# Fewer parts of q and k before the first head; the rest, a split of gate weights and a set of zeros among the heads

## The chip, the cores and the metric

One core of one Trainium2 chip. The metric is the device time of one execution in microseconds. A core's engines are TensorE (PE in the rows, with its weight loads as PEld), VectorE (DVE), ScalarE (ACT), GpSimd (POOL) and SyncE (SP), which here only issues DMA.

## The reference

Two layers, each attention-like mixing and then a feed-forward part, on x and a context of 8 batches of 256 rows by 256 columns. The change lies in the first mixing. Its q is the normalised x, its k and v are the context, with 8 heads of 32 columns:

```python
gate_in = jnp.concatenate([q, k, v], axis=-1)
ig = jnp.transpose(gate_in @ igate_w.T + igate_b, (0, 2, 1))
fg = jnp.transpose(gate_in @ fgate_w.T + fgate_b, (0, 2, 1))
log_f_cum = jnp.cumsum(jax.nn.log_sigmoid(fg), axis=-1)
log_fg_mat = log_f_cum[:, :, :, None] - log_f_cum[:, :, None, :]
log_D = jnp.where(ltr, log_fg_mat + ig[:, :, None, :], -jnp.inf)
max_log_D = jnp.max(log_D, axis=-1, keepdims=True)
D = jnp.exp(log_D - max_log_D)
qk = jnp.einsum('bhsd,bhtd->bhst', qh, kh) / jnp.sqrt(jnp.float32(dh))
C = qk * D
normalizer = jnp.maximum(jnp.abs(jnp.sum(C, axis=-1, keepdims=True)), jnp.exp(-max_log_D))
h = jnp.einsum('bhst,bhtd->bhsd', C / (normalizer + EPS_BACKEND), vh)
```

h is then normalised by head and added to x. Behind it come a mixture of 32 experts (4 a row) with a shared one, a long convolution of the context with two small feed-forward blocks, and 8 dense experts of four times that width.

## The kernel before

The first mixing is 64 heads, batch by batch (head i is head i % 8 of batch i // 8). For exactness q and k are taken as a high part (rounded to fp32r) and a low part (the rest). The tile `parts` holds both, of k first and then of q in the same place, in four groups of 512 rows, which are two batches or 16 heads each; a group has two halves c of 128 columns. ScalarE makes the high parts of k, VectorE those of q (line 566), GpSimd all low parts by a subtraction (line 1618). SyncE stores each finished group to HBM (`k_parts`, `q_parts`), and loads it back as stacks: one stack holds, for four heads, high, low, high of k beside high, high, low of q on 96 partitions, in six DMAs (`load_stack`, line 439), so that one matrix product (lines 1795 and 1796) gives the scores. A group makes four stacks, so 16 stacks in all; `stackA` and `stackB` hold two each. `stackB` lies where q transposed (`qT`) is kept, and the second half of `stackA` where the gates' weights are.

Ahead of the heads the opening normalises x (line 556), transposes context and x (TensorE, lines 1750), multiplies by the gates' weights (line 1756), and forms from the gates the rows of cumulated log gates on VectorE and ScalarE (lines 569 to 584, `rows_done` at the last). TensorE fills its wait with 42 products of no use (`spare`, line 1743), then transposes these rows (line 1783) and starts head 0.

In a head TensorE makes scores (lines 1795 and 1796) and the exponents' argument (line 1801), ScalarE the exponentials `Dm` (lines 1308 and 1309), VectorE the product of both `Cm` (line 645), and TensorE two heads later the values (lines 1810 to 1812). The scores of head i wait for `Cm` of head i - 2. VectorE has small work between products: `head_work` closes the batch before, GpSimd finishes it.

All DMAs of SyncE stand in one queue in program order. Through the heads they are the stacks and, between them, 16 stores of zeros (`slots_in`, line 461), which clear 12.6 MB of HBM for the experts' slots from two rows of `eS` that GpSimd set to zero at the start (line 1600). VectorE waits for the last of them behind its last product. `split_gates` (lines 588 to 596) splits weights that are first read behind the heads.

## Time and profile before

| | |
|---|---|
| median of 3 runs | 1803.57 us (1801.59 to 1806.38) |
| the profiled execution: time, span | 1809.64 us, 1807.6 us |
| busy: PE, DVE, ACT, POOL | 92%, 67%, 26%, 25% |
| mean granted TensorE clock | 0.959 |
| first scores of head 0, last of head 63 | 57.44 us, about 151 us |
| DMA, whole span | 127.49 MB, 71 GB/s |

The chain that ended last lies for 78% on TensorE and 39% on one line of the dense experts (1943), which the change does not touch. The opening and the heads are the first 155 us of the span. A clock of 1.00 in the rows is 2.4 GHz, 0.50 is 1.2 GHz. A row with xN merges N operations; its time goes from the first's start to the last's end.

### The profile page before, as it was taken

The page shows a single profiled execution, that of the slowest core. Times are in us where ns is not written, and L with a number is a line of the kernel's source. Part 1 is how long each engine was busy: PE and PEld are TensorE (multiplying, and loading weights), DVE is VectorE, ACT ScalarE, POOL GpSimd, SP SyncE. Part 2 cuts the span into 40 slices and gives each one's busy share as a digit, 9 for nine tenths or more (in the row PEclk, how much of TensorE's full clock was granted, in tenths as well). Part 3 has the DMA queues.
Part 4 walks back from the last instruction along what each step waited for, and adds up shares of the span by engine and source line. Part 5 has one row for each costly group of instructions (what it writes and reads, how often), then busy time and mean ns, then how long its engine had stood idle before and what let it go on. Part 6 is the DMA issues. An engine that isn't in the chain of part 4 may idle for free.

```text
span 1807.6 us, 28969 instructions
## 1 busy us (share of the span) xinstructions
PE 1665.6 (92%) x9720; PEld 1429.5 (79%) x9721; DVE 1209.2 (67%) x2472; ACT 478.8 (26%) x844; POOL 452.3 (25%) x299
## 2 busy tenths in 40 slices
PE   5998987698956698999999999999999999999998
PEld 5796663398844588888888888888888888888887
DVE  7556778566655695666676676676676676666765
ACT  3455331143422365321111121121211111211211
POOL 5152256688436511010010010010010110100100
PEclk9998998899977898999999999999999999999999
DMA  7992021378643200001000000010000010010001
GB/s 239 294 328 88 24 83 75 105 243 264 204 136 101 64 1 18 18 18 36 18 27 25 17 35 17 17 35 17 17 35 17 17 35 17 17 35 17 17 0 47
DMA packets 72002, 127.49 MB, mean 71 GB/s; under 512 B 8320, under 2 KB 51776, under 8 KB 71808
## 3 DMA queue, kind: packets, MB, share of 16 engines
q1 hardware_dynamic: 38096, 84.31, 14.3%
q10 hardware_dynamic: 27696, 25.51, 4.4%
q0 software_dynamic: 6144, 16.79, 2.9%
q8 instruction: 42, 0.69, 0.2%
q14 instruction: 24, 0.20, 0.0%
HBM read 82.54 MB, written 44.04 MB: 70 GB/s over the span
## 4 chain that ended last, share of the span: by engine, by line
PE 78%; DVE 7%; issue 4%; POOL 4%; DMA 4%; ACT 2%; another core or an unknown queue 1%; SPq 0%; POOLq 0%; DVEq 0%; ACTq 0%
PE ps L1943 39%; PE ps L1959 20%; PE ps L2050 4%; DMA slots_in<-xn,idS 2%; POOL slots_in L1672 2%; PE ps L2069 2%; PE ps L2125 1%; PE ps L1743 1%; PE ps L2147 1%; PE ps L2030 1%; DMA x<-in_x 1%; PE ps L1812 1%; PE ps L1811 1%; PE ps L2059 1%
## 5 line engine op out<-in xcount | busy, mean ns | idle before, releaser
L1943 PE MATMUL ps<-xTH,wH 128*128 128x512 f32 x1024 | 402.8, 393 | 1.6 <-DVE hF L1197 1.6
L1943 PE MATMUL ps<-xTH,wL 128*128 128x512 f32 x1024 | 402.2, 393 | 0.0
L1943 PE MATMUL ps<-xTL,wH 128*128 128x512 f32 x1024 | 399.1, 390 | 0.0
L1345 ACT ACTIVATE sg<-ps 128x512 f32<-128x512 f32 x264 | 157.9, 599 | 885.8 <-PE ps L1943 878.0
L1197 DVE TENSOR_TENSOR hF<-sg,ps 128x512 f32<-128x512 f32 x256 | 175.7, 686 | 304.0 <-ACT sg L1345 304.0
L1644 POOL TENSOR_TENSOR wL<-wS,wH 128x1536 fp32r<-128x1536 f32 x32 | 111.9, 3496 | 961.0 <-ACT wH L1340 961.0
L1959 PE MATMUL ps<-wL,hH 128*128 128x256 f32 x1024 | 289.8, 283 | 0.0
L1959 PE MATMUL ps<-wH,hL 128*128 128x256 f32 x1024 | 289.7, 283 | 0.0
L1959 PE MATMUL ps<-wH,hH 128*128 128x256 f32 x1024 | 288.6, 282 | 0.5 <-DVE hL L1206 0.5
L1206 DVE TENSOR_TENSOR hL<-hF,hH 128x512 fp32r<-128x512 f32 x256 | 258.0, 1008 | 0.1
L1943 PEld LDWEIGHTS ps<-xTL,wH 128*128 128x128 f32 x1024 | 192.8, 188 | 42.2
L1216 DVE SCALAR_TENSOR_TENSOR x<-ps,cw,x 128x256 f32<-128x256 f32 x512 | 222.6, 476 | 1.0 <-PE ps L1959 1.0
L1943 PEld LDWEIGHTS ps<-xTH,wH 128*128 128x128 f32 x1024 | 193.8, 189 | 35.6 <-ACT sg L1345 1.5
L1943 PEld LDWEIGHTS ps<-xTH,wL 128*128 128x128 f32 x1024 | 193.9, 189 | 30.5
L1959 PEld LDWEIGHTS ps<-wH,hH 128*128 128x128 f32 x1024 | 195.5, 191 | 10.6 <-DVE hL L1206 0.7
L1959 PEld LDWEIGHTS ps<-wH,hL 128*128 128x128 f32 x1024 | 195.5, 191 | 9.9
L1959 PEld LDWEIGHTS ps<-wL,hH 128*128 128x128 f32 x1024 | 195.5, 191 | 0.0
L1200 DVE CAST hH<-hF 128x512 fp32r<-128x512 f32 x256 | 109.3, 427 | 36.9 <-PE ps L1959 28.2
L1672 POOL DMA_INDIRECT slots_in<-xn,idS x64 | 74.9, 1170 | 61.0 <-DMA slots_in<-xn,idS 31.2
L2050 PE MATMUL ps<-eHL,hH 128*128 x384 | 82.2, 297 | 2.3 <-POOL eHL L1659 2.3
L1743 PE MATMUL ps<-maskT,idb 128*128 128x384 bf16 x308 | 67.2, 345 | 15.4 <-DVE x L939 15.4
L1711 POOL DMA_INDIRECT yg<-slots_out,idG x48 | 49.3, 1027 | 73.8 <-DMA slots_out<-yo 49.1
(387 smaller groups left out, 2469.0 us busy)
## 6 DMA issues: line engine op xcount, KB each, us to landing
wS<-in_w SPq DMA_DIRECT2D x32, 768.0 KB
slots_in<-eS SPq DMA_DIRECT2D x16, 768.0 KB, 8.5
eS<-in_wr SPq DMA_DIRECT2D x32, 384.0 KB, 3.8
xl<-slots_in ACTq DMA_DIRECT2D x48, 256.0 KB, 3.6
slots_out<-yo ACTq DMA_DIRECT2D x48, 256.0 KB, 2.7
k_parts<-parts SPq DMA_DIRECT2D x8, 512.0 KB, 4.4
q_parts<-parts SPq DMA_DIRECT2D x8, 512.0 KB, 5.0
stackA<-k_parts SPq DMA_DIRECT2D x24, 128.0 KB, 6.4
```

The costliest lines, as they stand in the source:

```text
L1197: dve.tensor_tensor(hF[:, b, :], sg[:, b, :], ps[:, 2 + b, :], ALU.mult).then_inc(mul_done, 1)
L1200: dve.tensor_copy(hH[:, b, :], hF[:, b, :]).then_inc(h_high, 1)
L1206: dve.tensor_tensor(hL[:, b, :], hF[:, b, :], f32(hH[:, b, :]), ALU.subtract).then_inc(h_low, 1)
L1216: dve.scalar_tensor_tensor(x[:, tile, :], acc, cw2[:, tile, bass.ds(it, 1)], x[:, tile, :], ALU.mult, ALU.add).then_inc(evac_done, 1)
L1345: act.activation(sg[:, b, :], ps[:, b, :], ACT.Silu).then_inc(silu_done, 1)
L1644: pool.tensor_tensor(blocks(wL, slot, plain), blocks(wS, slot, plain), f32(blocks(wH, slot, plain)), ALU.subtract).then_inc(w_low, 1)
L1672: pool.indirect_dma_start(xs_d, bass.IndirectOffsetOnAxis(ap=idS[:, n, k:k + 1], axis=0), xn[:, n, :], None, bounds_check=TILES * P - 1, o ...
L1711: pool.indirect_dma_start(slot_rows(n)[:, k, :], None, ys_d, bass.IndirectOffsetOnAxis(ap=idG[:, n, k:k + 1], axis=0), bounds_check=TILES ...
L1743: pe.matmul(ps[:, bank, 0:384], idb[:, :], maskT[:, :], start=True, stop=True)
L1943: last = pe.matmul(ps[:, 2 * half + b, :], piece(w, s, slot, col, P), v[:, k, g * 512:(g + 1) * 512], start=q == 0, stop=q == 5)
L1959: last = pe.matmul(o, h[:, b, t * P:(t + 1) * P], piece(w, s, slot, col, D), start=(opens and t % 2 == 0 and q == 0), stop=(closes and q = ...
L2050: last = pe.matmul(ps[:, 2 + b, t * D:(t + 1) * D], h[:, b, (2 * t + k) * P:(2 * t + k + 1) * P], eFlat[:, bass.ds(off + (w + k * D), D)], ...
```

## The change

Before the first head, only group 0 of q and k gets its low parts: those of k on GpSimd, those of q on VectorE itself right after the casts. GpSimd makes the low parts of k of groups 1 to 3 when the gate rows are done, and then those of q. VectorE makes the high parts of q of groups 1 to 3 behind the products of heads 5, 6 and 7, each pair behind a wait for that group's k stores. Stacks 2 and 3 get places of their own, `stackC` in `xn` and `stackD` in `eS`, so all four stacks of group 0 can be loaded before q transposed is free. `eS` is therefore set to zero only when the scores of head 15 are done. `split_gates` moves behind the product of head 14 and two small operations behind that of head 15. The column of means in `vext` is made group by group. SyncE's order follows.

```diff
@@ -143,6 +143,8 @@
         parts = at("parts", [P, 2, 2, NT * P], F32R, start["dcw"])
         stackA = at("stackA", [P, 2, 2, 4, SEQ], F32R, start["wS"])
         stackB = at("stackB", [P, 2, 2, 4, SEQ], F32R, start["xTH"])
+        stackC = at("stackC", [P, 2, 4, SEQ], F32R, start["xn"] + 4 * 8 * D)
+        stackD = at("stackD", [P, 2, 4, SEQ], F32R, start["eS"])
         qT = at("qT", [P, 2, NT * P], F32, start["xTH"])
         kT = at("kT", [P, 2, NT * P], F32, start["xTL"])
         xTM = at("xTM", [P, 2, NT * P], F32R, start["ya"])
...
@@ -390,6 +392,8 @@
 
         def stack(j):
 
+            if j in (2, 3):
+                return (stackC, stackD)[j - 2][:, :, :, :]
             return (stackA, stackB)[j % STACKS // 2][:, j % 2, :, :, :]
 
         def f32(ap):
@@ -438,26 +442,35 @@
                         src = of[i, :, c, b * SEQ:(b + 1) * SEQ].rearrange("(h d) t -> d h t", d=DH)
                         sp.dma_start(f32(stack(j)[r * DH:(r + 1) * DH, a, :, :]), src).then_inc(stack_loaded[j % STACKS], 16)
 
-            for g in range(4):
+            sp.wait_ge(k_low, 2)
+            store_parts(kp_d, 0, k_stored[0])
+            sp.wait_ge(q_low, 2)
+            store_parts(qp_d, 0, q_stored[0])
+            load_stack(0)
+            sp.wait_ge(gates_done, 1)
+            load_stack(1)
+            load_stack(2)
+            load_stack(3)
+            for g in range(1, 4):
                 sp.wait_ge(k_low, 2 * g + 2)
                 store_parts(kp_d, g, k_stored[g])
-            for g in range(4):
+            for g in range(1, 4):
                 sp.wait_ge(q_low, 2 * g + 2)
                 store_parts(qp_d, g, q_stored[g])
-                if g == 0:
-                    load_stack(0)
-            sp.wait_ge(gates_done, 1)
-            for j in range(1, STACKS):
-                load_stack(j)
-
-            sp.wait_ge(vext_done, 1)
+                if g == 1:
+                    load_stack(4)
+                    load_stack(5)
+            load_stack(6)
+            load_stack(7)
+
+            sp.wait_ge(vext_done, 4)
             for t, n in ((FZ, "fz"), (FW, "fw"), (Win, "win"), (peT, "pet"), (Wp1, "wp1"), (Wp2, "wp2")):
                 sp.dma_start(t[tuple(slice(None) for _ in t.shape)], dram[n]).then_inc(conv_loaded, 16)
             sp.wait_ge(zero_done, 1)
             zv = xs_d.rearrange("(a p c) d -> a p (c d)", p=P, c=UW // D)
             for a in range(TILES * D // UW):
-                if STACKS + a < 2 * B:
-                    load_stack(STACKS + a)
+                if 2 * STACKS + a < 2 * B:
+                    load_stack(2 * STACKS + a)
                 sp.dma_start(zv[a], eS[:, 0:2, :].rearrange("p i c -> p (i c)")).then_inc(zeros_stored, 16)
 
             sp.wait_ge(pv_done, B * NH)
@@ -554,16 +567,28 @@
             link(row_scales(range(4)))
             for n in range(NT):
                 dve.tensor_scalar(xn[:, n, :], x[:, n, :], mv[:, n, 0:1], rs[:, n:n + 1], ALU.subtract, ALU.mult).then_inc(norm_done, 1)
-            for g in range(4):
-                last = dve.tensor_reduce(vext[:, 4 * g:4 * g + 4, :, DH + 1], vext[:, 4 * g:4 * g + 4, :, 0:DH], AXX, ALU.add)
-                if g == 3:
-                    link(last)
-                    dve.tensor_scalar(vext[:, :, :, DH + 1], vext[:, :, :, DH + 1], 1.0 / DH, None, ALU.mult).then_inc(vext_done, 1)
+
+            def query_high(g):
+
                 dve.wait_ge(k_stored[g], 32)
                 for c in range(2):
                     cols_ = slice(g * 512, (g + 1) * 512)
                     dve.wait_ge(mixT_copied, 8 + 2 * g + c + 1)
                     dve.tensor_copy(parts[:, 0, c, cols_], qT[:, c, cols_]).then_inc(q_high, 1)
+
+            def head_means(g):
+
+                means = vext[:, 4 * g:4 * g + 4, :, DH + 1]
+                link(dve.tensor_reduce(means, vext[:, 4 * g:4 * g + 4, :, 0:DH], AXX, ALU.add))
+                dve.tensor_scalar(means, means, 1.0 / DH, None, ALU.mult).then_inc(vext_done, 1)
+
+            head_means(0)
+            query_high(0)
+            for c in range(2):
+                dve.wait_ge(q_high, c + 1)
+                dve.tensor_tensor(parts[:, 1, c, 0:512], qT[:, c, 0:512], f32(parts[:, 0, c, 0:512]), ALU.subtract).then_inc(q_low, 1)
+            for g in range(1, 4):
+                head_means(g)
             dve.wait_ge(gates_copied, 1)
 
             dve.scalar_tensor_tensor(r1[64:, :], rg[64:, :], -1.0, rg[64:, :], ALU.mult, ALU.min).then_inc(negabs_done, 1)
@@ -596,9 +621,6 @@
                 dve.scalar_tensor_tensor(zHL[:, :], f32(zHL[:, :]), ident[0:2, 0:1], low, ALU.mult, ALU.add).then_inc(bias_split, 1)
                 dve.wait_ge(bias_split, 1)
 
-            split_gates()
-            dve.tensor_scalar(tc[:, 0:1], nl[:, 0:1], -0.5, None, ALU.mult)
-            link(dve.tensor_scalar(tc[:, 4:9], tilen[:, 0:5], float(RING), float(RING), ALU.mult, ALU.add))
 
             def constant(k, shape):
 
@@ -645,6 +667,13 @@
                 dve.scalar_tensor_tensor(Cm[:, i % 3, :], ps[:, i % 2, 0:384], float(DH) ** -0.5, Dm[:, i % 2, :],
                                          ALU.mult, ALU.mult).then_inc(mixed_done, 1)
                 b = i // NH
+                if 5 <= i < 8:
+                    query_high(i - 4)
+                if i == 14:
+                    split_gates()
+                if i == 15:
+                    dve.tensor_scalar(tc[:, 0:1], nl[:, 0:1], -0.5, None, ALU.mult)
+                    link(dve.tensor_scalar(tc[:, 4:9], tilen[:, 0:5], float(RING), float(RING), ALU.mult, ALU.add))
                 if i >= 8 and i % 8 in (2, 3):
                     head_work(b - 1, i % 8 - 2)
                 if i >= 16 and i % 8 == 1:
@@ -1597,7 +1626,6 @@
                 pool.wait_ge(pool_step, steps[0])
 
 
-            pool.memset(eS[:, 0:2, :], 0.0).then_inc(zero_done, 1)
             link(pool.memset(zcol[:, :], 0.0))
             pool.wait_ge(ident_loaded, 16)
             pool.tensor_copy(idb[:, :], ident[:, :])
@@ -1609,17 +1637,21 @@
                 for a in range(2):
                     last = pool.tensor_copy(gateW[:, :, b, 64 * a + 8 * b:64 * a + 8 * b + 8], gwt[:, 0:4, 8 * a:8 * a + 8])
             last.then_inc(gatew_done, 1)
-            def low_parts(src, first, signal):
-
-                for j in range(8):
+            def low_parts(src, copied, first, last, signal):
+
+                for j in range(2 * first, 2 * last):
                     g, c = j // 2, j % 2
                     cols_ = slice(g * 512, (g + 1) * 512)
-                    pool.wait_ge(q_high if first else k_high, j + 1)
+                    pool.wait_ge(copied, j + 1)
                     pool.tensor_tensor(parts[:, 1, c, cols_], src[:, c, cols_], f32(parts[:, 0, c, cols_]), ALU.subtract).then_inc(signal, 1)
 
-            low_parts(kT, 0, k_low)
-            low_parts(qT, 8, q_low)
+            low_parts(kT, k_high, 0, 1, k_low)
             pool.wait_ge(const_loaded, 11 * 16)
+            pool.wait_ge(rows_done, 1)
+            low_parts(kT, k_high, 1, 4, k_low)
+            low_parts(qT, q_high, 1, 4, q_low)
+            pool.wait_ge(qk_done, 16)
+            pool.memset(eS[:, 0:2, :], 0.0).then_inc(zero_done, 1)
 
             def rows_of(ap):
                 return ap.rearrange("p s h -> p (s h)").unsqueeze(2).to_broadcast([P, 2 * NH, DH])
@@ -1806,6 +1838,7 @@
                 o0, o1 = (ps[:, 4 + 2 * (b % 2) + s, h * (DH + 2):(h + 1) * (DH + 2)] for s in range(2))
                 pe.wait_ge(mixed_done, i + 1)
                 if h == 0:
+                    pe.wait_ge(vext_done, b // 2 + 1)
                     wait(pe, head_read, b - 1)
                 pe.matmul(o0, Cm[:, i % 3, P:2 * P], vext[:, 2 * b, h, :], start=True, stop=True)
                 pe.matmul(o1, Cm[:, i % 3, 2 * P:3 * P], vext[:, 2 * b, h, :], start=True, stop=False)
```

On VectorE, at the end of the opening, before (`parts<-qT` are casts to the high parts, `vext` the head sums, `r_129<-rg` the first gate operation):

```order
L558 TENSOR_REDUCE vext<-vext 128x32
L566 CAST parts<-qT 128x512 x2
L558 TENSOR_REDUCE vext<-vext 128x32
L566 CAST parts<-qT 128x512 x2
L558 TENSOR_REDUCE vext<-vext 128x32
L566 CAST parts<-qT 128x512 x2
L558 TENSOR_REDUCE vext<-vext 128x32
L561 TENSOR_SCALAR vext<-vext 128x128
L566 CAST parts<-qT 128x512 x2
L569 SCALAR_TENSOR_TENSOR r_129<-rg 64x256
```

On VectorE at the same place, now:

```order
L582 TENSOR_REDUCE vext<-vext 128x32
L583 TENSOR_SCALAR vext<-vext 128x32
L577 CAST parts<-qT 128x512 x2
L589 TENSOR_TENSOR parts<-qT,parts 128x512 x2
L582 TENSOR_REDUCE vext<-vext 128x32
L583 TENSOR_SCALAR vext<-vext 128x32
L582 TENSOR_REDUCE vext<-vext 128x32
L583 TENSOR_SCALAR vext<-vext 128x32
L582 TENSOR_REDUCE vext<-vext 128x32
L583 TENSOR_SCALAR vext<-vext 128x32
L594 SCALAR_TENSOR_TENSOR r_131<-rg 64x256
```

Three of the four pairs of casts are gone from there, and two subtractions have come. On VectorE in heads 0 to 10, now (before, `Cm` stood there eleven times with nothing between):

```order
L609 CAST MHL<-r_132 64x256
L667 SCALAR_TENSOR_TENSOR Cm<-ps,Dm 128x384 x6
L577 CAST parts<-qT 128x512 x2
L667 SCALAR_TENSOR_TENSOR Cm<-ps,Dm 128x384
L577 CAST parts<-qT 128x512 x2
L667 SCALAR_TENSOR_TENSOR Cm<-ps,Dm 128x384
L577 CAST parts<-qT 128x512 x2
L667 SCALAR_TENSOR_TENSOR Cm<-ps,Dm 128x384 x3
```

The casts stand behind the products of heads 5, 6 and 7. On SyncE, from the first store of parts on, now (before, all stores of k and q stood ahead of stack 1):

```order
L431 DMA k_parts<-parts 256x1x512 x2
L431 DMA q_parts<-parts 256x1x512 x2
L443 DMA stackA<-k_parts 32x4x256 x3
L443 DMA stackA<-q_parts 32x4x256 x3
L443 DMA stackA<-k_parts 32x4x256 x3
L443 DMA stackA<-q_parts 32x4x256 x3
L443 DMA stackC<-k_parts 32x4x256 x3
L443 DMA stackC<-q_parts 32x4x256 x3
L443 DMA stackD<-k_parts 32x4x256 x3
L443 DMA stackD<-q_parts 32x4x256 x3
L431 DMA k_parts<-parts 256x1x512 x6
L431 DMA q_parts<-parts 256x1x512 x2
```

Six stores of k and six of q have moved behind the loads of stacks 0 to 3.

## Rows read from the trace of the kernel before

**Rows 1.** Stretches of 5 us: busy PE, PEld, DVE, ACT, POOL; clock, DMA share, GB/s.
```profile
60.00:65.00 5.00, 4.94 (x37) 3.99 (x35) 2.23 (x4) 2.45 (x7) 0.00 (x0) 0.90 1.07 245
...
105.00:110.00 5.00, 5.00 (x43) 4.61 (x43) 2.44 (x5) 2.76 (x8) 0.06 (x1) 1.00 1.07 362
...
135.00:140.00 5.00, 5.00 (x43) 4.48 (x42) 3.31 (x11) 2.74 (x8) 4.77 (x4) 1.00 1.02 424
```

**Rows 2.** Timeline of the opening: start, us busy, engine, line, tiles, idle before and releaser.
```profile
36.18 1.21 DVE L558 TENSOR_REDUCE vext<-vext 128x32 f32<-128x1024 f32 x1
...
44.07 2.90 DVE L566 CAST parts<-qT 128x512 fp32r<-128x512 f32 x2
...
45.35 0.47 ACT L1264 ACTIVATE rg<-ps,gbias 128x256 f32<-128x256 f32 x1 [2.72 <-PE ps L1756]
...
47.00 1.38 DVE L569 SCALAR_TENSOR_TENSOR r<-rg 64x256 f32<-64x256 f32 x1
...
50.58 0.42 DVE L571 SCALAR_TENSOR_TENSOR r<-rg,r 64x256 f32<-64x256 f32 x1 [2.20 <-ACT r L1268]
...
55.59 0.28 DVE L584 CAST MHL<-r 64x256 fp32r<-64x256 f32 x1
...
57.44 0.67 PE L1795 MATMUL ps<-stackA 96*128 96x256 f32 x1
...
60.99 0.39 PE L1795 MATMUL ps<-stackA 96*128 96x256 f32 x1
```

**Rows 3.** Busy time by stretches of 1 us, before the first head.
```profile
51.00:52.00 1.00, 1.00 (x7) 0.49 (x5) 0.69 (x1) 0.24 (x1) 0.00 (x0) 1.00 1.05 404
52.00:53.00 1.00, 0.14 (x1) 0.00 (x0) 0.76 (x2) 0.98 (x2) 0.00 (x0) 1.00 1.05 401
...
54.00:55.00 1.00, 0.00 (x0) 0.00 (x0) 0.92 (x4) 0.00 (x0) 0.00 (x0) 0.57 1.03 393
```

**Rows 4.** Timeline: low parts on GpSimd, and a pair of casts.
```profile
19.84 9.84 POOL L1618 TENSOR_TENSOR parts<-kT,parts 128x512 fp32r<-128x512 f32 x8 [10.00 <-ACT parts L1258]
...
37.30 0.75 DVE L566 CAST parts<-qT 128x512 fp32r<-128x512 f32 x2
37.80 11.71 POOL L1618 TENSOR_TENSOR parts<-qT,parts 128x512 fp32r<-128x512 f32 x8 [8.12 <-DVE parts L566]
```

**Rows 5.** Timeline of the kernel's start.
```profile
0.73 1.38 POOL L1600 MEMSET eS<- 128x1536 f32 x1 [0.29 <-POOLq L2301]
...
1.31 0.87 DVE L541 CAST one<-ones 2x128 fp32r<-2x128 f32 x1
```

**Rows 6.** Timeline of heads 53 to 55.
```profile
136.15 0.36 PE L1795 MATMUL ps<-stackA 96*128 96x256 f32 x1
...
137.78 1.28 POOL L1635 TENSOR_TENSOR hC<-hC,bcv 128x512 f32<-128x512 f32 x1
...
138.06 0.56 DVE L645 SCALAR_TENSOR_TENSOR Cm<-ps,Dm 128x384 f32<-128x384 f32 x1 [0.81 <-PE ps L1796]
...
139.10 0.36 PE L1795 MATMUL ps<-stackA 96*128 96x256 f32 x1
```

**Rows 7.** Timeline: first and last operation of the gate weights' split, eight in all.
```profile
55.90 0.20 DVE L588 CAST wg0H<-wg 128x64 fp32r<-128x64 f32 x1
...
57.85 0.47 DVE L596 SCALAR_TENSOR_TENSOR zHL<-zHL,ident,cmp 2x256 fp32r<-2x256 f32 x1
```

**Rows 8.** Timeline of SyncE's queue.
```profile
41.01 1.18 SPq L427 DMA_DIRECT2D q_parts<-parts  x2
45.51 1.30 SPq L439 DMA_DIRECT2D stackA<-k_parts  x3
```

**Rows 9.** Page, DMA issues: KB each, median us from issue to landing.
```profile
slots_in<-eS SPq DMA_DIRECT2D x16, 768.0 KB, 8.5
```

**Rows 10.** Timeline behind the heads.
```profile
158.18 0.17 DVE L535 SCALAR_TENSOR_TENSOR sd<-mv,rs 128x8 f32<-128x8 f32 x1
...
162.63 0.62 ACT L1281 ACTIVATE hQ<-hC 128x512 f32<-128x512 f32 x1
```

More of the change, by code:

```diff
@@ L229, in build @@
         assert end["Cm"] <= start["tF"] and end["kc"] <= end["tF"] and end["h1T"] <= start["Dm"] and end["id2"] <= end["cw2"]
-        assert end["parts"] <= end["ya"] and end["stackA"] <= start["FW"] and end["stackB"] <= end["xTH"]
+        assert end["parts"] <= end["ya"] and end["stackA"] <= start["FW"] and end["stackB"] <= end["xTH"] and end["stackC"] <= end["xn"] and end["stackD"] <= end["eS"]
         assert end["hC"] <= end["xn"] and end["hQ"] <= start["Dm"] and end["GI"] <= end["vext"] and end["WF"] <= end["eS"]
```

## The prediction

> **What bounds the kernel.** I read the stretches first, then the timeline of the opening, then its releasers. Through the heads TensorE is full (4.94 of 5 us at first, then 5.00), while the DMA engines are busy too, at 245 GB/s for loads of the stacks alone, 362 for stack loads and stores of zeros in turn and 424 for zeros alone [rows 1]. So what can be won is an earlier first head, and nothing in the heads, where each microsecond that TensorE waits is lost. What sets the first head is seen in [rows 2]. The gates' sums are copied out by ScalarE at 45.35 to 45.82, but VectorE still casts the last parts of q until 46.97 and takes up the gates (L569) only at 47.00. That operation lasts 1.38 us, and the next of the same shape 0.42 (L571). The last row of the gate chain ends at 55.87, and the first scores start at 57.44.
>
> Why 1.38: GpSimd makes low parts until 37.80 + 11.71 = 49.51 [rows 4]. Its eight of k, with no VectorE cast beside them, took 9.84, 1.23 each. A pair of VectorE casts that started at 37.30, ahead of GpSimd's first operation at 37.80, took 0.75; the pair at 44.07, with GpSimd in full run, took 2.90, so 1.45 for one cast [rows 2, 4].
>
> **The opening after the change.** VectorE's order is: sum of the first head group (1.21, [rows 2]) with its scaling, two casts (0.75), two low parts of q (I take 0.6 each: 512 columns against 0.42 for 256 of L571), then three more sums with scalings. The norms end with the row at 36.18, which starts there. 36.2 + 1.2 + 0.2 + 0.75 + 1.2 = 39.6, then three times 1.4 is 43.9, ahead of 45.82. So L569 starts when the gates are copied: 47.00 - 45.85 = 1.15 us won. GpSimd has nothing to do then, so it lasts 0.42 instead of 1.38: 0.96 won. The rest of the chain, 48.38 to 55.87, starts after that or lies beside an idle GpSimd from 49.51, and stays as it is. The rows are ready at about 53.8.
>
> The granted clock of TensorE was 1.00 (2.4 GHz) at 51 to 52 us and 0.57 in 54 to 55 [rows 3], so it fell to 1.2 GHz there, and the 0.90 of 60 to 65 [rows 1] says that it rose again soon after 60; before it fell, TensorE had run out of filling work near 52.1 (0.14 us busy in 52 to 53 [rows 3]) and waited for the rows until 55.9, 3.7 us. The wait shrinks to 1.6 us. What that does to the clock no row tells; I take it as staying up (55 in 100). At 1.2 GHz the scores of heads 0 and 2 started at 57.44 and 60.99 [rows 2]; two heads at full speed take 2 x 1.474 = 2.95 instead of 3.55, so 0.6 won, and nothing if the clock falls all the same. First head: 2.1 earlier, 2.7 with the clock.
>
> The first stack is no bar: before, the q store issued at 41.01 let the load start at 45.51, 4.5 us [rows 8]; now 39.65 + 4.5 = 44.2, first scores at 55.
>
> **The heads' slack on VectorE.** From 136.15 to 139.10 TensorE does two heads, 1.474 each; the product of the head that starts at 136.15 ends at 138.62, and the head two later needs it at 139.10 [rows 6]. So VectorE has 1.474 - 0.56 = 0.91 us free in a head and may then be 0.48 late. The product itself kept 0.56 with a GpSimd operation of 512 columns running (137.78 to 139.06) [rows 6], so the low parts of k under the first heads cost the products nothing.
>
> **Casts in heads 5, 6, 7.** GpSimd makes k's six remaining low parts from 53.8 to 53.8 + 6 x 1.23 = 61.2. With the first scores at 55.0 (57.44 - 2.1, and 0.35 that I allow for the transposes at full clock), head 5's product ends at T = 55.0 + 5 x 1.474 + 2.47 = 64.8. Its pair of casts finds GpSimd idle: 0.75, inside 0.91. But each pair releases two low parts of q (2.5 us), which are running when head 6's product ends at T + 1.47. There casts and low parts take turns as in the pair of 2.90: the running one ends at T + 2.0, a cast to 2.3, a low part to 3.5, a cast to 3.9. Head 7's product ends at T + 4.5, not T + 2.95: 1.55 late, less 0.48, holds TensorE 1.07. The third pair goes likewise from T + 4.5 to T + 7.0; head 8's product ends at T + 7.6, not T + 4.4: 3.2 late, less 0.48 is **2.7 us** in all. Bounds: 0 if no cast is held; 3.5 if both pairs take the full 2.90. I take 2.7, worked from the row with both.
>
> A rule bears on this: the Trainium skill, SBUF — State Buffer, section Who interferes with whom, says that VectorE's casts in their two-port mode and GpSimd hold one shared port pair as a lock for a whole instruction, and that whoever issues first decides who is blocked. By that, casts that come first cost 0.75 a pair and GpSimd pays; the pair at 37.30 shows such a case, and it would bring the sum to that of the second rival below.
>
> **Split of the gate weights in head 14.** Eight linked operations, 55.90 to 57.85 + 0.47 = 58.32: 2.42 us [rows 7], before the change beside waiting and free. Now it stands between two products. And the zeros (one set of 1.38 us) are made by GpSimd when head 15's scores are done, some 0.6 after they start, so at S + 2.1 if head 14 starts at S, until S + 3.45; head 14's product ends at S + 2.47. At the start of the kernel a VectorE cast of 2 rows took 0.87 and ended at 2.18, just behind that same set (0.73 to 2.11) [rows 5]. So the split's first cast waits 1.0. 1.0 + 2.42 - 0.91 - 0.48 = **2.0 us**. Bounds: 1.0 without the wait, 2.4 if the set ends as late as a whole 1.38 after the product. The two small operations in head 15 fit into 0.91. The sums' scaling, split in four, lies ahead of 45.82: nothing.
>
> **Transfers.** Order on SP: k and q of group 0, stacks 0 to 3, k of 1 to 3, q of 1, stacks 4 and 5, q of 2 and 3, stacks 6 and 7, the filter's six loads, then stacks and zeros in turn. A stack is 0.786 MB, 3.2 us at 245; a store pair 1.05 MB, 2.6 at 404 [rows 3]; zeros 1.85 at 424. Four stacks from 45.0 end at 58. k's pairs, ready at 56.3, 58.7 and 61.2, are through at 60.6, 63.4 and 66, stored near 68 for the last; head 7 wants it at T + 4.5 = 69.3. q of group 1: low parts done at T + 3.6 = 68.4, stored 72.9, stack 4 landed near 78 against head 16 at 55.0 + 23.6 + 2.7 = 81.3. Queue from 73.8: stacks 4 and 5 (6.4), q of 2 and 3 (5.2), stacks 6 and 7 (6.4), filter (2.3 MB, 7 at 332 as an estimate between 245 and 424), stack 8 (3.2) end at 102; head 32 starts at 107. Then eight pairs at 4.35 and eight zeros at 1.85 end near 151. VectorE waits for the zeros after its last product, but there it has room: it ended its next work at 158.35 while ScalarE, which needs it, only got to its square at 162.63 [rows 10]. All hidden, the nearest by 1.3 us (k of group 3), 3.3 (stack 4) and 5 (stack 8).
>
> **Sum.** -1.15 - 0.96 - 0.6 + 2.7 + 2.0 = +2.0 us, rounded; behind the heads TensorE is next on the chain, so it passes on whole. The profiled execution took 1809.64 for a span of 1807.6; it becomes 1811.6. The median shown, 6.1 below, becomes 1805.6. A change of 0.3% (5.4 us) is about what a measurement of this kernel can tell from none, so this is no change.
>
> **Rivals.** (1) Forecast, both stalls as above: 50 in 100; own range 1802 to 1809, from the lower bounds of the stalls with the clock up (-2.7 + 1.0 = -1.7, 1801.9) to the upper with the clock down (-2.1 + 5.9, 1807.4), and 1.5 for the scatter of the runs (1801.59 to 1806.38). (2) The casts come first and GpSimd pays: the pairs fit, the split alone stays: -2.7 + 1.0 = -1.7, 1801.9. For it: the pairs at 37.30 (0.75). Against: in heads 6 and 7 low parts are surely running. 25 in 100. (3) Slower: the new wait of VectorE for k's stores in heads 5 to 7. These stores stand behind 24 stack loads in one queue. Landing took 8.5 us at the median for zeros in a full queue [rows 9]; if group 3 takes 12 from its issue at 61.4, it comes at 73.4, 4.1 behind head 7, and the sum is +6.1: 1809.7. It decides from a landing at 69.3 on, one to one; past 0.3% from 72.7. Against it: the DMA work ahead ends at 66. 15 in 100, two thirds of it past 0.3%. (4) The opening gains nothing, because the gates or the first stack come later than I have them: TensorE's first head stays at 57.4 and the stalls add 4.7: 1808.3. 10 in 100.
>
> **Range and chances.** 1800 to 1811: it leaves out part of (3), and for (2) what scatter takes below. Faster by over 0.3% needs (2) with 3.7 more from scatter: 0.08. Slower: 0.10 from (3), 0.04 from (1) and (4): 0.14. Same: 0.78.
>
> **What will show it.** L569's successor starts at 45.9 and lasts 0.42; first scores at 55.0; granted clock of 1.00 throughout 54 to 61. Casts in head 5 last 0.4, in heads 6 and 7 over 1; gaps of TensorE before the scores of heads 9 and 10 sum to 2.7, before head 17 to 2.0, with the first split cast near 1.1 long. The heads end 2 us later than before; zeros near 151. Wrong if a VectorE wait names the k stores, if a stack load ends a TensorE wait, or if the stalls break the clock and the half-speed stretch moves into the heads.

## The result, and the profile after

| | before | after |
|---|---|---|
| median of 4 runs | 1804.82 us (1801.59 to 1806.38) | 1871.14 us (1869.11 to 1874.21) |
| the profiled execution: time, span | 1809.64, 1807.6 | 1870.7, 1868.4 |
| mean granted TensorE clock | 0.959 | 0.924 |
| first scores of head 0 | 57.44 | 46.94 |
| last scores of head 63 | 150.88 | 212.17 |

The ratio is 1.0371, with an interval of 1.035 to 1.0393: 3.7% slower, where 1805.6 and no change were forecast. The first head came 10.5 us earlier, and the last 61.3 later.

The first place to look is the clock. Here are the 20-us windows of the changed kernel (busy time of PE, PEld, DVE, ACT and POOL, each with its number of instructions, then the granted clock, DMA share, GB/s):

```profile
60.00:80.00 20.00, 17.92 (x83) 15.63 (x82) 9.23 (x21) 5.44 (x15) 6.59 (x5) 0.60 0.87 273
80.00:100.00 20.00, 20.00 (x88) 17.65 (x87) 9.37 (x22) 5.52 (x17) 6.55 (x4) 0.50 0.89 240
...
200.00:220.00 20.00, 20.00 (x82) 17.07 (x81) 9.13 (x23) 4.90 (x13) 6.12 (x4) 0.50 0.06 19
220.00:240.00 20.00, 16.47 (x53) 8.96 (x51) 11.88 (x44) 11.86 (x21) 0.00 (x0) 0.72 0.12 48
```

TensorE is busy for 20.00 of 20 us, which looks like a full engine, but it gets through 88 products in 20 us where the kernel before got through 43 in 5 [rows 1]. Its clock is 0.50, 1.2 GHz, from 63.84 to 227.68. DMA share is 0.06 at 200, so no transfer holds it. The 1-us windows show where the clock fell:

```profile
60.00:61.00 1.00, 0.23 (x2) 0.20 (x2) 0.75 (x2) 0.21 (x1) 0.97 (x1) 1.00 0.28 107
...
62.00:63.00 1.00, 0.47 (x5) 0.35 (x4) 1.00 (x2) 0.64 (x2) 0.64 (x2) 1.00 1.02 383
63.00:64.00 1.00, 0.22 (x1) 0.23 (x2) 1.00 (x3) 0.00 (x0) 1.00 (x1) 0.92 0.65 236
64.00:65.00 1.00, 1.00 (x6) 0.66 (x6) 0.19 (x1) 0.00 (x0) 1.00 (x2) 0.50 0.00 0
```

TensorE did nothing from 62.47 to 63.78, ahead of the fall at 63.84, and VectorE and GpSimd were both full from 63 on. That is the place of the casts, in the timeline of the heads (start, us busy, engine, line, tiles; in brackets the idle time before and who ended it):

```profile
56.55 0.76 DVE L577 CAST parts<-qT 128x512 fp32r<-128x512 f32 x2
57.06 2.61 POOL L1646 TENSOR_TENSOR parts<-qT,parts 128x512 fp32r<-128x512 f32 x2 [3.63 <-DVE parts L577]
...
58.40 0.36 PE L1827 MATMUL ps<-stackC 96*128 96x256 f32 x1
59.00 1.28 DVE L577 CAST parts<-qT 128x512 fp32r<-128x512 f32 x2 [1.09 <-DMA k_parts<-parts]
...
60.80 0.39 PE L1827 MATMUL ps<-stackC 96*128 96x256 f32 x1 [0.77 <-DVE Cm L667]
61.53 1.72 DVE L577 CAST parts<-qT 128x512 fp32r<-128x512 f32 x2 [0.79 <-DMA k_parts<-parts]
...
63.78 0.56 PE L1827 MATMUL ps<-stackC 96*128 96x256 f32 x1 [1.31 <-DVE Cm L667]
66.57 0.56 PE L1827 MATMUL ps<-stackC 96*128 96x256 f32 x1
```

Heads 8, 9 and 10 start at 58.40, 60.80 and 63.78, distances of 2.40 and 2.98 where 1.474 is the rule [rows 6]: 0.93 and 1.51, together 2.4 us, lost to the casts. From 63.78 on a head takes 2.80 us, to 212.17 at head 63.

A third wait, of 0.74 us ahead of head 2, belongs to the start of the heads: the first product waits there for the first exponentials. It is also in runs without the change (0.77 in the first one below), and the clock kept at 1.00 behind it.

The sum of the heads: the start is 10.5 earlier. From head 0 to head 10 it takes 16.84, before 15.35 (2 heads of 1.775 and 8 of 1.474): +1.5, the 2.4 less what the first two heads save (2.59 now, 3.55 before). From head 10 to head 63 it takes 148.4 instead of 53 x 1.474 = 78.1: +70.3. Together +61.3, and the span grew by 60.8.

The opening after, in the timeline, answers to [rows 2]:

```profile
22.82 0.17 DVE L521 TENSOR_TENSOR nt<-rs 128x16 f32<-128x16 f32 x1
...
24.92 5.26 DVE L569 TENSOR_SCALAR xn<-x,mv,rs 128x256 f32<-128x256 f32 x16
...
37.44 0.47 ACT L1293 ACTIVATE rg<-ps,gbias 128x256 f32<-128x256 f32 x1 [2.72 <-PE ps L1788]
37.95 0.42 DVE L594 SCALAR_TENSOR_TENSOR r<-rg 64x256 f32<-64x256 f32 x1 [0.47 <-ACT rg L1293]
...
45.59 0.28 DVE L609 CAST MHL<-r 64x256 fp32r<-64x256 f32 x1
...
46.94 0.36 PE L1827 MATMUL ps<-stackA 96*128 96x256 f32 x1
```

The same stretch of the kernel before, rows that were not shown ahead:

```profile
27.31 1.18 DVE L510 SCALAR_TENSOR_TENSOR rs<-nt,rs 128x16 f32<-128x16 f32 x1
...
29.75 0.17 DVE L509 SCALAR_TENSOR_TENSOR nt<-nt,ve 128x16 f32<-128x16 f32 x1
...
31.00 5.26 DVE L556 TENSOR_SCALAR xn<-x,mv,rs 128x256 f32<-128x256 f32 x16
```

Before, normalisation of x started at 31.00, now at 24.92. The small operations ahead of it, on 16 columns, last 0.17 each when GpSimd is idle, and up to 1.19 beside its low parts of k, about one of GpSimd's operations of 1.23 [rows 4]. This run of small operations took 8.1 us before and 2.5 now: 5.6 of the 10.5. The other parts: 0.5 earlier at its start; 1.8 from the start of `xn` to the copy of the gates (14.35 before, 12.52 now; TensorE waited 6.05 us for `xn` before and was at half clock from 30.25 to 37.08, now it waited 0.44 and 0.20 and kept its clock); 1.15 less wait for L569's successor (1.65 to 0.51); 0.96 in that operation; 0.5 from the rows to the scores (1.57 to 1.07).

### The profile page after: what moved, and what is told of

It is laid out like the page before. It is cut to its first block, busy times and chain, and to the rows that moved or that the text cites. A ratio compares the mean times of both kernels' runs of the same rounds, so it can differ in the third digit from the quotient of the medians.

```text
span 1868.4 us, 28976 instructions
## 1 busy us (share of the span) xinstructions
PE 1733.6 (93%) x9720; PEld 1487.5 (80%) x9721; DVE 1213.8 (65%) x2477; ACT 477.9 (26%) x844; POOL 452.6 (24%) x297
## 4 chain that ended last, share of the span: by engine, by line
PE 79%; issue 5%; DVE 4%; POOL 3%; DMA 3%; ACT 2%; POOLq 0%; DVEq 0%; SPq 0%; another core or an unknown queue 0%; ACTq 0%
PE ps L1976 38%; PE ps L1992 19%; PE ps L2083 4%; DMA slots_in<-xn,idS 3%; PE ps L1775 2%; PE ps L2102 2%; POOL slots_in L1704 2%; PE ps L2180 2%; PE ps L2158 1%; PE ps L1844 1%; PE ps L1845 1%; PE ps L2063 1%; PE ps L1827 1%; PE ps L1833 1%; PE ps L1843 1%
## 5 line engine op out<-in xcount | busy, mean ns | idle before, releaser
L1775 PE MATMUL ps<-maskT,idb 128*128 128x384 bf16 x308 | 85.4, 411 | 15.7 <-DVE x L968 15.7
L667 DVE SCALAR_TENSOR_TENSOR Cm<-ps,Dm 128x384 f32<-128x384 f32 x64 | 35.6, 557 | 96.4 <-ACT Dm L1338 88.0
```

Source lines behind the costliest of these rows:

```text
L1775: pe.matmul(ps[:, bank, 0:384], idb[:, :], maskT[:, :], start=True, stop=True)
```

## The experiments

The kernel before took 1793.8, 1792.6 and 1792.7 us beside these runs, on three chips, about 0.6% less than the 1804.82 above; so each run is given as a ratio to the kernel before on the same chip. Of the slower variants and of the burst there are two executions each and one trace, while the kernel before scatters from 1788 to 1801 by itself. My theory: waits of some 2 us that fall together are enough to drop the clock in the heads, and once it is down it does not come back, whatever caused the waits. Rivals: GpSimd's and the DMAs' new neighbours make the heads themselves slower; or only the casts do it.

**Does a wait alone do it? Four, two and three idle sums in the kernel before.** This edit puts nothing of the change into the kernel before, only sums of no use behind head 8's product (here four, in the others 2 and 3):

```diff
@@ kernel before, VectorE's heads @@
                 b = i // NH
+                if i == 8:
+                    for _ in range(4):
+                        link(dve.tensor_reduce(cmp8[:, 0:4, :], vext[:, 0:4, :, 0:DH], AXX, ALU.add))
```

> The kernel before with one delay added: behind the product of head 8 VectorE does four more sums of 1.21 us each that nobody reads. Theory A (the clock has two self-holding states in the heads: a head at 1.2 GHz takes 2.80 us and TensorE, though always busy, does not get back to 2.4 GHz): TensorE waits 3.7 us before head 10, its granted clock falls to 0.50 and stays there to the end of the heads, 54 heads x (2.80 - 1.474) = 72 us, so about 1880 us. Theory B (a stall costs itself and one short half-speed stretch, as 54 to 61 us in the kernel before; the changed kernel is slow for another reason, such as its transfers): 3.7 + 3 us, about 1811 us.

Measured: 1872.91 us, ratio 1.0442 (1.042 to 1.0463). The waits of TensorE by releaser (us, times, the longest), and a window behind them:

```profile
PE ps L1798 <- DVE Cm L645: 4.2, 2, 3.4
```

```profile
80.00:100.00 20.00, 20.00 (x88) 17.65 (x87) 5.39 (x14) 5.83 (x16) 1.41 (x1) 0.50 0.82 254
```

One wait of 3.4 us, before head 10 (the other, of 0.8, is the one ahead of head 2), costs 79 us. The window reads like that of the changed kernel at the same time, down to the 88 products, with GpSimd at 1.41 us instead of 6.55: its work in the heads does not keep them slow. The low clock lasted from 75.75 to 239.59. So a wait of VectorE's making is enough, with none of the change's casts, stores or places. It is longer than those of the changed kernel; how small a wait may be was asked next.

Two sums:

> The kernel before, with two idle sums of 1.21 us behind the product of head 8 instead of four: TensorE waits 2.5 - 0.91 - 0.48 = 1.1 us once. If the clock falls only when TensorE has missed enough in one place (theory A1), it stays at 2.4 GHz and the time is the kernel before's plus 1.1 us. If any gap in the heads tips it (A2), it falls as with four sums and the time is 70 us longer.

Measured: 1792.92 us, ratio 1.0001 (0.9982 to 1.002).

```profile
PE ps L1798 <- DVE Cm L645: 0.9, 1, 0.9
```

The clock stayed up: a wait of 0.9 us costs less than can be measured. Three sums:

> The kernel before with three such sums: a wait of 2.4 us, as much as TensorE lost before heads 9 and 10 of the changed kernel together. Theory A (the loss of 66 us is this stall and what the clock makes of it): the clock falls to 0.50 until the end of the heads and the time is about 73 us longer. Rival: 2.4 us are too little by themselves, the changed kernel's other differences are needed; then 2.4 us longer, or at most 5 with a short half-speed stretch.

Measured: 1870.08 us, ratio 1.0432 (1.0391 to 1.0474). Waits, then windows of 10 us:

```profile
PE ps L1798 <- DVE Cm L645: 2.2, 1, 2.2
```

```profile
70.00:80.00 10.00, 7.84 (x58) 6.87 (x56) 7.66 (x14) 3.23 (x9) 0.00 (x0) 0.90 1.05 309
80.00:90.00 10.00, 10.00 (x44) 8.78 (x45) 2.23 (x4) 3.15 (x9) 0.00 (x0) 0.50 1.07 333
```

One wait of 2.2 us is enough, and GpSimd is idle in both windows. The clock was still 1.00 in the microsecond to 78 and 0.50 in the next, so it fell 1.6 us after the wait had ended at 76.39. Between 0.9 and 2.2 us of wait the price goes from nothing to 77 us. It is a step; where it lies is not sharp, as later runs show.

**Is the price that of the heads left? Three sums behind head 40.** The same edit with `if i == 40` and `range(3)`.

> The kernel before with the three idle sums of 1.21 us behind head 40 instead of head 8. Theory A (from the stall on every head takes 2.80 instead of 1.474 us until the heads end): 2.2 + 21 x 1.33 = 30 us longer than the kernel before, against 78 behind head 8. Rival (the loss does not depend on the heads that are left, for instance because stacks and zeros fall out of step): about as much as behind head 8.

Measured: 1822.9 us, ratio 1.018 (1.0149 to 1.0211), so +30.2 us. Windows before and behind it:

```profile
100.00:120.00 20.00, 20.00 (x166) 18.30 (x163) 12.37 (x35) 10.89 (x29) 11.41 (x8) 1.00 1.04 340
...
130.00:150.00 20.00, 20.00 (x88) 17.48 (x87) 5.97 (x13) 5.63 (x15) 6.42 (x5) 0.50 0.66 253
```

166 products in 20 us against 88, both with TensorE at 20.00. A wait of the same kind (2.27 us, ahead of head 42) costs 30 here and 77 behind head 8, since the loss is paid per head that is left, some 22 against 54 at 1.33 each.

**Can the clock be had back? A burst in head 20 of the changed kernel.** The casts and their waits stay.

```diff
@@ kernel after, TensorE's heads @@
-                spare(2 + i % 2, 2)
+                spare(2 + i % 2, 26 if i == 20 else 2)
```

> The changed kernel, and in head 20 alone TensorE does 26 instead of 2 of the filling products (bf16, 384 columns, dense), which are overwritten. Theory A: the dense burst of some 8 us lifts the clock to 1.00 near head 20 and it stays there; heads 20 to 63 take 1.474 us instead of 2.80, so 44 x 1.33 - 8 = 50 us less than the changed kernel, about 1821 us, unless a late stack makes TensorE wait again and the clock falls a second time. Theory B (the clock is held down by something that goes on through the heads, such as VectorE's or the queue's work): the clock falls back at once, about 1871 + 7 = 1878 us.

Measured: 1804.5 us, ratio 1.006 (1.004 to 1.008), against 1.0371 for the changed kernel. The timeline around it:

```profile
88.74 0.56 PE L1827 MATMUL ps<-stackA 96*128 96x256 f32 x1
91.54 0.56 PE L1827 MATMUL ps<-stackA 96*128 96x256 f32 x1
92.01 6.78 PE L1775 MATMUL ps<-maskT,idb 128*128 128x384 bf16 x26
...
99.50 0.36 PE L1827 MATMUL ps<-stackA 96*128 96x256 f32 x1
100.98 0.36 PE L1827 MATMUL ps<-stackA 96*128 96x256 f32 x1
```

Heads are 2.80 apart ahead of the burst and 1.48 behind it. Work of no use for 6.8 us takes more than 50 us off the time, in ratio 0.031 of 1793.8, or 56 us; the clock stayed up from about 96.8 to the end of the heads. So the slow state is not a property of these heads' work, neighbours or buffers: the heads behind the burst are the same as in the changed kernel and ran at full speed. The rival of slower heads falls.

**Is it the casts alone? One cast a head.** The pairs behind heads 5, 6 and 7 are taken apart and put behind heads 6, 7, 8, 9, 12 and 13.

```diff
@@ kernel after, VectorE's heads; `only` picks the halves of a pair @@
-                if 5 <= i < 8:
-                    query_high(i - 4)
+                if i in (6, 7, 8, 9, 12, 13):
+                    j = (6, 7, 8, 9, 12, 13).index(i)
+                    query_high(1 + j // 2, (j % 2,))
```

> The changed kernel with its six casts of q spread one to a head (heads 6, 7, 8, 9, 12, 13), so that none waits for a k store or for a low part on GpSimd. Theory A: no wait of TensorE before head 14. What comes then is the split of the gate weights behind head 14 (up to 2.0 us) and stack 4, which landed near 70 us while head 16 would start at 70.2. If the clock survives these, about 1800 us; if it falls there, the heads from 17 on take 2.80 us: 47 x 1.33 = 62, about 1860 us. Theory B: no large difference from 1871 us, and the half-speed stretch starts at 64 us as before.

Measured: 1854.4 us, ratio 1.0339 (1.0293 to 1.0384). In the execution with a trace (1848.2 us; the other took 1860.6 and has none) no wait came from the casts, and the clock passed their place; it fell at 72.34 instead, at the next fault:

```profile
69.74 0.61 DVE L613 CAST wg0H<-wg 128x64 fp32r<-128x64 f32 x1
...
70.64 1.06 DVE L615 CAST wg1HL<-wg 128x32 fp32r<-128x32 f32 x1
...
72.19 0.42 PE L1828 MATMUL ps<-stackA 96*128 96x256 f32 x1 [1.73 <-DMA stackA<-q_parts]
```

TensorE waited 1.73 for stack 4 ahead of head 16, a wait that the changed kernel never shows because its heads are slow by then; the clock fell 0.15 us after it ended. Two casts of the gate weights' split stand beside the set of zeros and last 0.61 and 1.06; the first lasted 0.20 before [rows 7]. But the split held TensorE for nothing here: its length lies within the wait for stack 4. The only other wait in the heads, 0.7 us, is the one ahead of head 2, and not the split's. A half-speed kernel hides later faults.

**And the split taken out.** As before, with six of the split's eight operations in VectorE's waits for the gate chain, the other two behind heads 14 and 15:

```diff
@@ e3_casts, VectorE's gate chain and heads @@
+            link(dve.tensor_copy(wg0H[:, :, :], wg0[:, :, :]))
+            link(dve.tensor_tensor(wg0L[:, :, :], wg0[:, :, :], f32(wg0H[:, :, :]), ALU.subtract))
...
             dve.wait_ge(softplus_done, 2)
...
                 if i == 14:
-                    split_gates()
+                    link(dve.tensor_scalar(low, low, ident[0:2, 1:2], None, ALU.mult))
```

> The changed kernel with casts in heads 6, 7, 8, 9, 12, 13 as in e3_casts, and the gate weights' split taken out of head 14 too (into the gaps of the gate chain, its last two operations singly behind heads 14 and 15). What is left of the waits in the heads is stack 4: in e3_casts it landed 1.7 us after TensorE wanted it at head 16. Theory A: that wait alone, with the one of stack 4 being 1.7 us, lies between 0.9 (held) and 2.2 us (fell) in the kernel before with idle sums. If it holds, about 1785 us; if it falls, 48 heads x 1.33 = 64 us more, 1849 us. The first would say that the two waits together (1.7 and 0.7 us) made the fall in e3_casts, the second that the order of SyncE's transfers is a fault of the change by itself.

Measured: 1839.56 us, ratio 1.0273 (1.0177 to 1.0368). The text on record counts 0.7 us of wait to the split; as said above, that wait stands ahead of head 2 and is in this run too. The scores that waited for a stack:

```profile
71.85 0.35 PE L1825 MATMUL ps<-stackA 96*128 96x256 f32 x1 [1.55 <-DMA stackA<-q_parts]
...
94.48 0.36 PE L1825 MATMUL ps<-stackB 96*128 96x256 f32 x1
...
99.56 0.55 PE L1825 MATMUL ps<-stackA 96*128 96x256 f32 x1 [3.44 <-DMA stackA<-q_parts]
```

Windows of 5 us between and behind them:

```profile
75.00:80.00 5.00, 5.00 (x42) 4.48 (x42) 4.08 (x12) 2.33 (x7) 3.15 (x2) 1.00 1.00 346
...
100.00:105.00 5.00, 5.00 (x24) 4.33 (x23) 0.56 (x1) 1.46 (x4) 0.00 (x0) 0.50 1.08 332
```

In this execution (1832.6 us) the clock survived 1.55 us alone, and fell at 97.92 in the wait of 3.44 for stack 8. The other execution took 14 us more and has no trace, so whether its clock outlasted stack 4 is not known. The order of SyncE's transfers is a second fault that drops the clock by itself.

**More filling work in every head.** Three filling products a head in the changed kernel instead of two (`spare(2 + i % 2, 3)`).

> The changed kernel with three filling products a head instead of two. Theory A in the form that TensorE at 1.2 GHz does too little dense work per time in a head to be lifted: the clock still falls near 64 us, as the stalls are the same, but it comes back within some 10 us, because a third of the filling more stands in each head; then 64 x 0.17 = 11 us for the filling at full clock, and the time is some 1871 - 67 + 11 = 1815 us. If the share of filling does not matter, the heads stay at 1.2 GHz and take 0.33 us more each: 1892 us.

Measured: 1868.63 us, ratio 1.0424 (1.0386 to 1.0463).

```profile
60.00:80.00 20.00, 17.21 (x134) 14.93 (x133) 12.99 (x30) 8.11 (x23) 7.60 (x6) 1.00 0.84 273
80.00:100.00 20.00, 20.00 (x85) 16.47 (x85) 7.76 (x15) 5.01 (x14) 6.55 (x4) 0.50 1.04 284
```

What stood ahead of the fall:

```profile
74.23 1.00 DVE L613 CAST wg0H<-wg 128x64 fp32r<-128x64 f32 x1
...
78.10 0.39 PE L1827 MATMUL ps<-stackA 96*128 96x256 f32 x1 [1.34 <-DVE Cm L667]
```

A miss on both sides: the clock outlasted the casts at 64, whose waits were 0.30 and 1.15 here, but it fell at 80.02 and did not come back, with a head at 3.12 us. One product more in each head is not what the burst was. What held TensorE here is the split behind head 14, at full clock: from 74.23 to 77.45, its first cast 1.00 long beside the set of zeros, and a wait of 1.34 before head 17. The clock fell 1.9 us after the end of that wait. So 1.34 us stood ahead of a fall here, and 1.55 did no harm in the run without the split: between 0.9 and 2.2 us the length of a wait alone does not decide. What else counts no run shows.

**Was the gain of the opening GpSimd's low parts? Those moved alone.** In the kernel before, GpSimd's low parts of k of groups 1 to 3 wait until x is normalised:

```diff
@@ kernel before, GpSimd's low_parts @@
+                    if not first and j == 2:
+                        pool.wait_ge(norm_done, NT)
```

> The kernel before with one part of the change's opening: GpSimd makes the low parts of k of groups 1 to 3 only when the norms are done; all casts, stores and loads stay in the opening. Theory O (the opening was held by VectorE's small norm operations waiting for GpSimd's low parts, 1.19 us instead of 0.17 each): these are 0.17 again and the norms end 5.6 us earlier. But the casts of q now run beside the low parts of k and wait for k stores some 9 us later than before, so the first scores come only 2 to 4 us earlier; about 3 us less than the kernel before. Rival: the norm operations are slow for another reason; no change.

Measured: 1792.98 us, ratio 1.0001 (0.9979 to 1.0022). The timeline:

```profile
22.72 0.17 DVE L508 TENSOR_TENSOR nt<-rs 128x16 f32<-128x16 f32 x1
...
37.33 0.47 ACT L1264 ACTIVATE rg<-ps,gbias 128x256 f32<-128x256 f32 x1 [2.72 <-PE ps L1758]
...
37.42 2.19 DVE L566 CAST parts<-qT 128x512 fp32r<-128x512 f32 x2 [3.18 <-DMA k_parts<-parts]
...
46.74 1.37 DVE L569 SCALAR_TENSOR_TENSOR r<-rg 64x256 f32<-64x256 f32 x1
...
57.18 0.67 PE L1797 MATMUL ps<-stackA 96*128 96x256 f32 x1
```

The first step held: the small operations last 0.17, the normalisation starts at 24.82, 6.2 earlier, and the gates are copied at 37.33, 8.0 earlier and as early as in the changed kernel. Then it is lost again, and of the 3 us that were expected nothing is left: the casts of q wait 3.18 for the k stores, which come later, and take 7.8 in all beside GpSimd's low parts instead of 5.2, so L569 starts at 46.74 (47.00 before). It needs both halves of the change: fewer low parts early, and no casts of q behind them.

**Is the idea worth something without the waits? First try.** The changed kernel with single casts (heads 1, 2, 4 to 7), the low parts of k right after the normalisation, the split in the waits of the gate chain, and stores and loads of SyncE in the order in which they are wanted (the filter's loads last). Its GpSimd part:

```diff
@@ kernel after, GpSimd @@
             low_parts(kT, k_high, 0, 1, k_low)
-            pool.wait_ge(const_loaded, 11 * 16)
-            pool.wait_ge(rows_done, 1)
+            pool.wait_ge(norm_done, NT)
             low_parts(kT, k_high, 1, 4, k_low)
```

> The changed kernel's opening, with all that made TensorE wait in the heads taken away: GpSimd makes the low parts of k of groups 1 to 3 right after the norms (30 us), the casts of q stand one to a head (1, 2, 4, 5, 6, 7), the split of the gate weights stands in the two gaps where VectorE waits for ScalarE in the gate chain, and SyncE issues the k stores after stack 0 or 1 and the filter's loads in the middle of the zeros. Theory A: first scores at 47 us, every head 1.474 us, granted clock 1.00 through the heads, last scores near 139.5 instead of 150.9, so 1804.8 - 11.4 = about 1793 us. Theory B (the early start itself overruns the transfers): stacks or zeros end waits of TensorE or VectorE and it lands above 1805 us.

Measured: 1787.58 us, ratio 0.9966 (0.9952 to 0.998), -6.2 us of the 11.4 expected. The clock was 0.50 when the heads began and 1.00 from 55.1 on, to their end. But the low parts of k now lay beside VectorE's own work of the opening:

```profile
31.84 2.96 DVE L582 CAST parts<-qT 128x512 fp32r<-128x512 f32 x2
...
50.83 0.28 DVE L625 CAST MHL<-r 64x256 fp32r<-64x256 f32 x1
```

A pair of casts at 2.96 instead of 0.75 [rows 4], and the last row ends at 51.1 instead of 45.9; the first scores started at 52.7. More than half of the opening's gain (4.8 us are left of 10.5) was paid back to GpSimd.

**Second try.** As that one, but only k of group 1 is made before the rows, after the low parts of q of group 0; casts in heads 3, 4, 6 to 9; the last two operations of the split behind heads 14 and 15, the two small ones behind head 16. SyncE's order follows.

```diff
@@ kernel after, GpSimd @@
             low_parts(kT, k_high, 0, 1, k_low)
+            pool.wait_ge(q_low, 2)
+            low_parts(kT, k_high, 1, 2, k_low)
             pool.wait_ge(const_loaded, 11 * 16)
             pool.wait_ge(rows_done, 1)
-            low_parts(kT, k_high, 1, 4, k_low)
+            low_parts(kT, k_high, 2, 4, k_low)
```

> As e4_no_stall, but GpSimd makes only group 1 of k's low parts ahead of the gate chain (behind the low parts of q of group 0) and groups 2 and 3 once the gate rows are done; casts of q in heads 3, 4, 6, 7, 8, 9; the last three small operations of the split stand singly behind heads 14, 15 and 16; SyncE's order follows. In e4_no_stall the casts and the gate chain waited for GpSimd's low parts and the first scores came at 52.7 us, with the clock at 0.50 before them. Theory A: first scores at 47 to 48 us, no wait in the heads over 0.5 us, granted clock 1.00 to the end of the heads; 5 to 6 us less than e4_no_stall, so 0.6% less than the kernel before. Rival: the stacks now come too late for the earlier heads, TensorE waits for one by more than 1 us and the clock falls: over 1830 us.

Measured: 1781.8 us (median of 12 runs), ratio 0.9945 (0.993 to 0.996): 10.8 us faster than the kernel before on the same chip, the best of all. First and last scores, and a window; the clock was 1.00 from there to the end of the heads:

```profile
47.01 0.36 PE L1832 MATMUL ps<-stackA 96*128 96x256 f32 x1
...
139.53 0.36 PE L1832 MATMUL ps<-stackB 96*128 96x256 f32 x1
```

```profile
60.00:80.00 20.00, 20.00 (x164) 18.19 (x163) 14.29 (x34) 10.34 (x29) 9.83 (x7) 1.00 0.88 265
```

The last head starts at 139.53, 11.4 ahead of the 150.88 of the kernel before. One wait of 0.75 us is left, the one ahead of head 2, with no harm. The casts and most of the low parts are made under the heads as in the changed kernel; their grain and place, the place of the split and SyncE's order differ, and by the two ratios the time differs by 4.3%.

## Why the prediction was wrong

**The step that failed** is the first sentence on the heads: "each microsecond that TensorE waits is lost". I priced a wait at its own length. The waits came out near in size (for the casts by chance, see below), and their price did not: 2.4 us of them cost 70 us more, since they dropped the clock and it stayed down. The text named this ("the stalls break the clock and the half-speed stretch moves into the heads") as what would make it wrong, but gave it no price and no chance, and spoke of a stretch: it took a low clock for a matter of some 7 us, as in 54.14 to 60.97 before. The rows of before gave the length of a head at either clock (1.774 in the first two, at half clock and with less work in them, and 1.474 in later ones); they did not show that the low state lasts. What they did show is that TensorE lost its clock in 3.7 us without work ahead of the heads; I did not ask the same of the 2.7 us of waits that I put into them. The Trainium skill, TensorE: Matmul & The Clock Gate, section HAM oscillation — how this bites in real kernels, says that waits between blocks of work can put the array back to its half clock, so that the next block starts slow; this was the rule that spoke against the change, and the traces bear it out; the waits in that section's example are some 3 to 5 us long, and here one of 2.2 us was enough. By its section What's actually happening sustained work releases the throttle again; the burst agrees, but through the heads TensorE is 20.00 of 20 us busy at 0.50 for 160 us, and there the measurement decides.

**The opening, -2.7: a term mis-sized.** The first scores came 10.5 earlier, and heads 0 and 1 took 1.0 less (0.6 forecast), so it measured -11.5. -1.15 and -0.96 came as worked out (0.42 for L569's successor, its wait shorter by 1.14). Missing was what GpSimd's low parts of k did to VectorE ahead of them: "The norms end with the row at 36.18, which starts there" took the place of the norms as fixed, although the rows beside it were 1.18 long where 0.17 was possible. That is 5.6 us; 1.8 more came from TensorE's clock, and 1.0 in two small pieces. The Trainium skill, SBUF — State Buffer, section Who interferes with whom, says that a VectorE operation with two inputs in SBUF also contends with a GpSimd operation that reads it; 0.17 against 1.18 agrees. I used that page for casts alone. So rival 4 (the opening gains nothing) was wrong by its sign.

**Casts, +2.7: measured 2.4, near by chance.** The first pair took 0.76, for 0.75 forecast. Of the second and third, 1.09 and 0.79 were waits for the k stores, which is rival 3's mechanism, and the casts took 1.28 and 1.72. With their waits that is 2.37 and 2.51 behind the product, where the forecast had 2.4 and 2.5 from turns with GpSimd and no wait at all. "All hidden" failed there: for group 3 VectorE was ready 8.6 us sooner than forecast (60.74 for 69.3), and the store came only 6.5 sooner (61.53 for 68). A VectorE wait that names the k stores was one of the signs of being wrong, and it came. Rival 2 ("The casts come first") did not come about.

**Split, +2.0:** in the changed kernel it is covered by slow heads and can't be read. In the kernel with single casts it lies within the wait for stack 4. With three filling products it can be read at full clock: the first cast 1.00 long (near 1.1 forecast), and a wait of 1.34, in heads that are 0.16 us longer each and so give it more room. The term was near.

**Transfers:** the times were near (stack 8 forecast by 102; it ended TensorE's wait at 99.56 in the run without the split), and the need was not: heads from 47 at full speed want it at 96.1, not at 107. The margin of 5 us was a wait of 3.44, that of stack 4, 3.3 us, one of 1.55. In that run head 16 wanted its stack at 70.3, 11.0 sooner than forecast, 8 of it from the opening and 2.7 from casts that no longer held it, and the stack landed 6.2 sooner; for stack 8 it was 10.9 against 2.4.

**Clock up in 54 to 61:** as forecast, 1.00 until 63.8. **Zeros near 151:** not so, with heads to 212 and nine of the sixteen stores of zeros issued from 170.8 on.

What stays open is what in a head keeps the clock down, and what besides its length makes a wait of 1 to 2 us drop it. The kernel before came back to 1.00 at 60.97 in its first heads; a third filling product in each head did not bring it back; 26 in a row did. No run here varied the kind of work in a head at the low clock alone.

## What to carry to other kernels

Ask of a wait that you add in a stretch where TensorE is full not only how long it is but whether the clock falls in it, and price that by the work that is left in the stretch: here 0.9 us cost nothing and 2.2 us cost 77, and in between 1.55 us passed where 1.34 did not, so trust only a single wait as short as those that always passed. Put moved work in pieces that fit the slack of one head, and reckon the margins of transfers from the start that the change gives, not from the old one. Read TensorE's busy share together with the granted clock and the number of products, since a share of 100% can be half speed.

## What was not expected of the hardware

- Two states that hold themselves: the same heads run at 1.474 us with the clock at 1.00, and at 2.80 with it at 0.50, each to the end of the heads if no longer wait or burst comes, and TensorE is 100% busy in both.
- What changes the state: one wait of 0.9 or 1.55 us did not, one of 1.34 (with three filling products a head), 1.73 or 2.2 us did; of waits two heads in a row, 0.30 and 1.15 did not, 0.77 and 1.31 did. The fall came inside the wait or up to 1.9 us behind its end. 26 filling products in 6.8 us brought the clock back.
- Operations of 16 columns on VectorE took 1.18 us instead of 0.17 beside GpSimd's subtractions of 1.23: the smallest operations pay about the whole length of a GpSimd instruction.
- The kernel before took 1804.8 us beside the changed kernel and 1792.6 to 1793.8 on three chips later; no run shows why.
